# Last attention: the keys' cosine and sine tables built by GpSimd at the head of the stage, not by VectorE

## The reference

```python
def _rope(x, pos):
    inv_freq = 1.0 / THETA ** (jnp.arange(0, HD, 2, dtype=jnp.float32) / HD)
    freqs = pos.astype(jnp.float32)[:, None, :, None] * inv_freq
    emb = jnp.concatenate((freqs, freqs), axis=-1)
    return x * jnp.cos(emb) + _rotate_half(x) * jnp.sin(emb)
...
q = _rms_norm(q, q_norm_w).transpose(0, 2, 1, 3)
kv_in = jnp.concatenate([context_hidden, draft_hidden], axis=1)
k = (kv_in @ Wk.T).reshape(bsz, total_len, KVH, HD)
v = (kv_in @ Wv.T).reshape(bsz, total_len, KVH, HD).transpose(0, 2, 1, 3)
k = _rms_norm(k, k_norm_w).transpose(0, 2, 1, 3)
full_position_ids = jnp.concatenate([context_position_ids, draft_position_ids], axis=1)
q = _rope(q, draft_position_ids)
k = _rope(k, full_position_ids)
...
scores = jnp.einsum('bhqd,bhkd->bhqk', q, k) * SCALE
probs = jax.nn.softmax(scores, axis=-1)
attn = jnp.einsum('bhqk,bhkd->bhqd', probs, v)
```

## Time and profile before

| | us |
|---|---|
| median of 3 runs | 1423.28 |
| lowest and highest of them | 1421.91, 1423.67 |
| the profiled execution, its own time | 1422.72 |
| its span, first to last instruction | 1420.9 |
| TensorE busy in the span | 1213.9 (85%) |
| VectorE busy | 864.1 (61%) |
| ScalarE busy | 605.6 (43%) |
| GpSimd busy | 342.0 (24%) |
| mean granted TensorE clock | 0.911 of full speed |

### The profile page before, as it was taken

One profiled execution on the slowest core, in us unless ns is written; L12 is line 12 of the kernel. 1 busy time (PEld: TensorE's weight loads), 2 busy tenths in 40 slices (PEclk: granted clock), 3 DMA queues, 4 the chain that ended last, 5 costly groups with the idle time before them and its releaser, 6 DMA issues.

```text
span 1420.9 us, 23408 instructions
## 1 busy us (share of the span) xinstructions
PE 1213.9 (85%) x8627; PEld 858.7 (60%) x8627; DVE 864.1 (61%) x1859; ACT 605.6 (43%) x1319; POOL 342.0 (24%) x280
## 2 busy tenths in 40 slices
PE   1685686999974998989999978999987999999986
PEld 0454364444433565688988744555556888888844
DVE  6777796777775551445555675333347776666566
ACT  2533252566652332344343232333334766555443
POOL 1313001222213001022222043445421232222222
PEclk9755798999965999989999979999999999999998
DMA  7100003500004113200000051111021000000010
GB/s 236 75 2 2 0 1 123 227 1 2 2 1 167 59 56 126 99 1 1 1 1 1 16 191 34 56 44 44 22 84 41 1 1 1 1 1 1 1 45 30
DMA packets 32163, 63.98 MB, mean 45 GB/s; under 512 B 5216, under 2 KB 23392, under 8 KB 30144
## 3 DMA queue, kind: packets, MB, share of 16 engines
q1 hardware_dynamic: 31296, 60.56, 12.0%
q0 software_dynamic: 768, 2.10, 0.4%
HBM read 54.91 MB, written 9.70 MB: 45 GB/s over the span
## 4 chain that ended last, share of the span: by engine, by line
PE 63%; DVE 16%; issue 5%; ACT 3%; POOL 2%; DMA 1%; DVEq 0%; SPq 0%; POOLq 0%; ACTq 0%
PE psum L1482 8%; PE psum L2191 4%; PE psum L2544 4%; PE psum L2582 4%; PE psum L2163 4%; PE psum L1464 4%; PE psum L2554 3%; PE psum L1788 3%; PE psum L2526 2%; PE psum L1138 2%; PE psum L2506 2%; PE psum L2116 2%; PE psum L2883 2%; PE psum L2094 2%; PE psum L1806 2%
## 5 line engine op out<-in xcount | busy, mean ns | idle before, releaser
L1299 DVE TENSOR_REDUCE c_max<-psum 128x2 f32<-128x512 f32 x128 | 81.5, 677 | 21.7 <-PE psum L1113 20.5
L1199 ACT ACTIVATE c_probs<-psum 128x512 f32<-128x512 f32 x128 | 75.2, 603 | 43.9 <-PE psum L1124 43.9
L1525 ACT ACTIVATE m_h_hi<-m_h 128x512 bf16<-128x512 f32 x50 | 31.5, 629 | 143.2 <-DVE m_h L1567 123.0
L1590 POOL TENSOR_TENSOR m_h_lo<-m_h,m_h_hi 128x512 bf16<-128x512 f32 x50 | 61.4, 1228 | 111.2 <-ACT m_h_hi L1525 111.1
L1482 PE MATMUL psum<-ctxT_yT_hi,m_w_hi 128*128 128x512 bf16 x200 | 78.0, 390 | 6.0 <-DVE m_h L1541 6.0
L1562 DVE TENSOR_TENSOR m_silu_up<-psum,m_silu 128x512 f32<-128x512 f32 x44 | 30.4, 691 | 80.0 <-PE psum L1482 79.7
L1482 PE MATMUL psum<-ctxT_yT_hi,m_w_lo 128*128 128x512 bf16 x200 | 78.0, 390 | 0.0
L1482 PE MATMUL psum<-ctxT_yT_lo,m_w_hi 128*128 128x512 bf16 x200 | 77.6, 388 | 0.0
L2582 PE MATMUL psum<-a_wo,a_outT 128*128 128x256 f32 x256 | 75.1, 405 | 0.7 <-DVE x_tok L2766 0.7
L2191 PE MATMUL psum<-a_wo,a_outT 128*128 128x256 f32 x256 | 75.2, 407 | 0.0
L2649 ACT ACTIVATE a_probs<-psum,a_max,a_q_rstd 128x128 f32<-128x128 f32 x128 | 56.8, 457 | 17.8 <-DVE a_max L2711 17.6
(11 more groups left out here) (498 smaller groups left out, 3454.1 us busy)
## 6 DMA issues: line engine op xcount, KB each, us to landing
m_w<-m_w SPq DMA_DIRECT2D x8, 1536.0 KB, 16.6
m_w<-m_w SPq DMA_DIRECT2D x27, 384.0 KB, 3.1
a_wq<-a_wq SPq DMA_DIRECT2D x2, 2048.0 KB
a_wo<-a_wo SPq DMA_DIRECT2D x2, 2048.0 KB, 11.3
a_trig<-trig_sin_cos SPq DMA_DIRECT2D x1, 2048.0 KB, 6.3
ctxT_yT_hi<-f_gate_up SPq DMA_DIRECT2D x2, 1024.0 KB, 7.4
a_sin_cos<-a_trig SPq DMA_DIRECT2D x1, 2048.0 KB, 9.7
m_rows<-m_zeros SPq DMA_DIRECT2D x1, 1920.0 KB, 13.7
```

The source lines that it names most:

```text
L1199: e.activation(c1P[:, n % 8, :, :], ps[:, 2 + n % 2, :].rearrange("p (k t) -> p k t", k=2), ACT.Exp, scale=float(1.0 / np.sqrt(np.float32( ...
L1299: e.tensor_reduce(c1M[:, u % 2, j, :], ps[:, c1_score_bank(n), :].rearrange("p (q t) -> p q t", q=2), AX.X, ALU.max).then_inc(c1_mx, 1)
L1590: e.tensor_tensor(hl[:, n_ % hb, :], hf[:, n_ % hb, :], hh[:, n_ % hb, :], ALU.subtract).then_inc(s_hl, 1)
```

## The change

VectorE's three table instructions go away. GpSimd gets five instructions ahead of its slots: a memset of a new tile `a3neg` (64 columns), a subtraction that makes it minus the row of norm weights (so the sign is in the row and no longer in the product), the cosine table of 2048 elements a partition, and the two halves of the sine table of 1024 each. The last three raise a semaphore that an earlier stage had left at 3 (`f0_q`), and `keys_rotated(0)` waits until all three are done. The values in the tables are the same.

```diff
         a3mx = m("a3_max", [P, 3, 4], F32)
+        a3neg = m("a3_minus_row", [P, 64], F32)
         a3sm = m("a3_sums", [P, 3, 4], F32)
...
         a3_op, a3_o = a3_sem("outT_in_psum"), a3_sem("outT_ready")
+        a3_kt = Turn(f0_q, 3)
...
-            def key_table(r):
-                sin, cos = (a3tr[:, 0, x, :].rearrange("p (b t) -> p b t", b=B) for x in range(2))
-                if r == 0:
-                    ins = e.tensor_tensor(a3kc[:, :, :].rearrange("p b (a t) -> p b a t", a=2), bc(cos, 2, 2),
-                                          bc(a3row[:, 1, :].rearrange("p (a t) -> p a t", a=2), 1, B), ALU.mult)
-                else:
-                    e.scalar_tensor_tensor(a3ks[:, :, 0:64], sin, -1.0, bc(a3row[:, 2, 0:64], 1, B), ALU.mult, ALU.mult)
-                    ins = e.tensor_tensor(a3ks[:, :, 64:128], sin, bc(a3row[:, 2, 64:128], 1, B), ALU.mult)
-                dve_step(e, ins)
...
             def keys_rotated(b):
                 v4 = "p (j a t) -> p j a t"
+                if b == 0:
+                    e.wait_ge(*a3_kt.at(3))
                 e.wait_ge(*a3_k2.at(b + 1))
...
-                if n in (-5, -4):
-                    key_table(n + 5)
...
             pool_step(e, e.memset(a3half[:, :], -0.5))
+            pool_step(e, e.memset(a3neg[:, :], 0.0))
+            e.wait_ge(*a3_in.at(48))
+            pool_step(e, e.tensor_tensor(a3neg[:, :], a3neg[:, :], a3row[:, 2, 0:64], ALU.subtract))
+            sin, cos = (a3tr[:, 0, x, :].rearrange("p (b t) -> p b t", b=B) for x in range(2))
+            e.tensor_tensor(a3kc[:, :, :].rearrange("p b (a t) -> p b a t", a=2), bc(cos, 2, 2),
+                            bc(a3row[:, 1, :].rearrange("p (a t) -> p a t", a=2), 1, B), ALU.mult).then_inc(a3_kt.sem, 1)
+            e.tensor_tensor(a3ks[:, :, 0:64], sin, bc(a3neg[:, :], 1, B), ALU.mult).then_inc(a3_kt.sem, 1)
+            e.tensor_tensor(a3ks[:, :, 64:128], sin, bc(a3row[:, 2, 64:128], 1, B), ALU.mult).then_inc(a3_kt.sem, 1)
```

## The result

The changed kernel takes 1427.55 us (median of 20 runs, 1424.06 to 1433.04) against 1423.20 us before (20 runs): a ratio of 1.0031, with an interval of 1.0018 to 1.0044, that is 2.6 to 6.3 us slower. A second comparison (12 runs against 35) gave 1.0020, 1.0003 to 1.0037. The prediction said 1423.7 us and no change.

What follows compares the result with a forecast made beforehand. TensorE bounds a3, waiting on VectorE at its head; removing VectorE's tables is nearly paid back by turn-taking with GpSimd, net +0.4 us, median 1423.7 us and no change. Range 1420.8 to 1426.2 us.

Steps and rivals of the forecast that it cites:

- Where the time is lost: Head of a3: TensorE waits 5.16 us for VectorE's keys of batch 0; time lost ahead of it carries to the end.
- the two engines take turns: Head of a3: VectorE and GpSimd block each other on the shared SBUF port; a held 512-element product ends 0.54 us after GpSimd.
- which VectorE instructions are held: Head of a3: L2723 and L2726, both inputs in SBUF, take turns with GpSimd; L2722, one input in PSUM, goes free.
- the new wait in front of the keys' rotation: VectorE's wait for GpSimd's tables before rotating keys, claimed to cost nothing.
- Which engine gets the port between L2687 and L2688: Between VectorE's two query tables (L2685, L2686 before): VectorE taken to finish both first; no row showed which wins.
- the slower rival: GpSimd takes the port before VectorE's second query table, so queries 0 start 2.3 us later; +1.7 us.
- the course that I took: Head of a3: VectorE finishes both query tables, then alternates with GpSimd; +0.4 us, chance 0.61 with -1.2 to +1.7.
- The prices on GpSimd: GpSimd's tables, scaled from smaller instructions: cosine 4.38 us, each sine half 2.29; 4.25 and 2.16 when queued.
- The ceiling of 1.45 us: Head of a3: most that removing VectorE's tables can gain, since queries 3 wait for ScalarE's last copy; 1.45 us.
- The clock, taken at zero: TensorE's half-speed stretches after the a3 gaps: the second may change either way, 1.7 us of uncertainty, counted as zero.
- the first gap's stretch: TensorE's 3.40 us at half speed after the 5.16 us gap, expected to stay with the gap about 4 us.
- rival 2: The lock starves the head of a3: +1.7 us, or +3.4 with one more half-speed stretch, which had chance 0.12.

Runs made afterwards that it cites:

- f_tables_wait: Changed kernel with GpSimd's tables waiting for VectorE's two query tables, plus fillers in TensorE's waits; a3 ended 285.58 us behind the first column product, no ratio given.
- f_before: Kernel before with filler matmuls keeping TensorE busy in its waits at the head of a3; 1419.61 us, 0.9976 of the kernel before.
- after_third: Changed kernel profiled a third time, nothing altered; a3 ended 291.12 us behind the first column product, no ratio given.
- f_after: Changed kernel with filler matmuls keeping TensorE busy in its waits at the head of a3; 1421.66 us, 0.9993 of the kernel before.

## Why the prediction was wrong

- **Where the time is lost, that the two engines take turns, and which VectorE instructions are held: right.** The zip stands in the timelines, the product on PSUM goes free, a held 512-element product ends 0.55 us after GpSimd (0.54 was summed), and the new wait in front of the keys' rotation cost nothing (the last table ends at 1079.02, and VectorE comes to the wait only at about 1086.3).
- **Which engine gets the port between L2687 and L2688: wrong**, and this is the step that turned the forecast. The sum let VectorE finish both query tables with GpSimd queued behind; the three executions of the changed kernel all show GpSimd getting in between, with 5.0 us for L2688. I had marked that as open, given it as the slower rival and priced it at +1.7 us. Its path was the right one as well: it had TensorE's queries 3 12.1 us behind the column product and VectorE's 15.9, measured are 12.31 and 16.24. Measured without the clock the cost is 1.97 us, against 1.14 us for the course that I took (E of f_tables_wait less E of f_before).
- **The prices on GpSimd: a bit low.** The cosine table took 4.39 us from the end of L2687 and 4.53 where nothing held it (so waiting does save the 0.14 us that was taken off), a sine half 2.21; the sum had 4.25 and 2.16. The course that I took costs 1.1 us and not 0.4: of the 0.7 us missing, some 0.4 are these prices (8.93 against 8.57), 0.2 the handing over from VectorE to GpSimd (1.86 us behind the column product and not 1.67), and the rest is small.
- **The ceiling of 1.45 us: right.** H fell by 1.59 us (0.14 beyond it) and E by 1.30 with small tables first and full clock. The time does not resolve it.
- **The clock, taken at zero: wrong.** The forecast had the first gap's stretch stay at 3.4 us. In all three executions of the changed kernel it was 6.8 us, and E came 1.5 us later for it. In the kernel before it was 6.8 us in one of three executions, so how much of this the change brings about and how much is chance is not settled. The gap itself was shorter (3.63 us, not 5.16), but TensorE had also stood idle for 0.87 to 1.04 us ahead of queries 3, and 2.13 ahead of queries 2 in after_third; that these gaps lengthened the stretch is not shown. I had allowed rival 2 with a further stretch 0.12 and +3.4; that is the size that came, +3.4 in E, but not quite the same course: the rival had a new stretch from the new gaps, and what came was the old one at double length.
- **The range** ended at 1426.2, 1.4 us below the median. It left out half a microsecond of rival 2 with its stretch, the course that came nearest.

That the difference of the medians (4.35 us) is above the 3.4 us in E lies inside its interval. Whether some executions lose more than these profiles show stays open.

## What to carry to other kernels

Moving work from VectorE to GpSimd is no free offload where VectorE meanwhile has instructions with two SBUF inputs, or long ones with a single SBUF input: each one queued then waits for a whole GpSimd instruction, and the trace shows it as busy time with a duration several times its usual one. If it must be moved, cut it in pieces (H 2.2 us better here) or let it start behind the VectorE instruction on which the most hangs (0.8 us better); both together were not tried. Better, look for idle time on VectorE itself and build first only what is needed first: 1.3 us in E here, though not resolved in the time. Where TensorE waits a few microseconds in several places, compare kernels with those waits filled: here the clock moved the end of the stage by 3 to 8 us between like kernels with and without fillers, and hid or nearly doubled a cost of 2.

## What the runs showed of the hardware that I had not expected

- GpSimd, queued behind one VectorE instruction, goes ahead of the next one even where VectorE has no wait between the two: the second query table was held for 4.3 us in all three executions of the changed kernel and in f_after. The Trainium skill (SBUF — State Buffer, section SBUF: two separate sides) says that the one that starts first gets the pair for the whole instruction; the trace agrees for these products (L2688 ended 0.55 us behind the whole cosine table), and the 16 pieces show that the turn is given up after each instruction.
- A half-speed stretch at the head came in 5 of the 9 executions without fillers at about 1.9 us ahead of the first column product, always 6.8 us long, and in neither kernel always. In the one execution of the kernel before that had it E was 1.4 us later; in the changed kernel E was the same with and without it (291.08, 291.13 and 291.12).
- Filling TensorE's three waits in a3 took every half-speed stretch out of it in four of five executions, and 3.2 us out of E of the kernel before (287.66 to 284.44). The kernel before with fillers is faster than it was without: 0.9976, 0.9954 to 0.9997.
